# First stage of a fused layer kernel reordered: seven weight chunks moved into the heads, values of tile 0 beside tile 1, one projection piece a step

## Chip, cores, metric

One NeuronCore of a Trainium2 chip (trn2). The metric is the device time of one execution in microseconds (us); the lower, the better. Time before: 1879.2 us, the median of 3 runs (1876.68 to 1882.17).

## The reference

```python
# attention, 16 heads of width 16, two score maps a head
s1 = q1 @ k1.T * scale;  s2 = q2 @ k2.T * scale        # (B=2, H=16, S=2048, S)
a1 = softmax(causal(s1));  a2 = softmax(causal(s2))
lam = exp(sum(lq1*lk1)) - exp(sum(lq2*lk2)) + LAM_INIT
out = (a1 - lam * a2) @ v                              # v of width 32
normed = (out - mean) * rsqrt(var + eps) * (1 - LAM_INIT)
x = layernorm(x + merge(normed) @ Wo)
# feed-forward, ternary weights with a scale for each row
h = silu(lin(x, w1)) * lin(x, w2)
h = gelu(lin(h, h1));  h = gelu(lin(h, h2))
x = layernorm(x + lin(h, w3))
```

x has 2 x 2048 tokens of 256, all in float32; the hidden width is 1024.

## The kernel before, in words

The 4096 tokens are eight tiles of 512. There are three stages: the projection of the first four pairs of heads and of all values; sixteen heads of attention; the rest of the layer, tile by tile. Each engine has its own program, and semaphores tie them together. Nothing is scheduled by a planner: the order is written out by hand.

**First stage** (`project_programs`, from L188). The loops of every engine run over the tiles t = 0..7 and over the pairs m = 0..3. Exact products come from float32r matmuls in three passes (high x high, low x high, high x low), so each input is cut into a high half (ScalarE, `high_x`, L371) and a low half (VectorE, `low_x`, L415). TensorE runs six matmuls for a pair (L525) and, where `value_tiles(t, m)` says so, six for a block s of values (L535). ScalarE copies the pair into one of six `copies` (L389), once the DMAs that read this buffer have landed and VectorE has measured it, and copies the values into `v_sb` (L401), once the store of the values two tiles ago has landed. VectorE takes the largest magnitude (L464). At pairs 2 and 3 it cuts the stacks of the tile before into their halves (`cut_piece`, L566 and L568), for which that tile's placements must have landed, and then runs `low_x(t + 1)`. SyncE's queue, in this order: a store of the pair to `qk_raw` (L309); for pair 0 also twelve placements of 32 KB into the stacks of head 0 (L319); at the end of the tile one load of an early chunk of the feed-forward weights (L291, tiles 0 to 4) and the store of `values` (L326, 1 MB). The loads of xt for later tiles (L282) are issued by ScalarE.

The feed-forward weights are 22 chunks of 128 x 1024. They are rounded to float32r and compared with the original, so that the kernel can tell whether rounding loses anything. Seven early chunks are rounded in the first stage (ScalarE L405, VectorE `compare`, L424); the other fifteen as thirty half chunks in the heads, two a head (`load_half` on SyncE, L1005; `round_half` on VectorE, L1384 and L1386). There is a single staging buffer for halves: `load_half(n)` waits until half n - 1 is compared.

**Heads** (`attention_programs`). A head has four query tiles, and its work is 36 steps: steps 0 to 2 belong to tile 0, 3 to 9 to tile 1, 10 to 20 to tile 2, 21 to 35 to tile 3. For each step TensorE computes the scores (L1196) into one of three PSUM slots, ScalarE the exponentials (L1152), GpSimd the mask on the diagonal, and three steps later TensorE weighs the values with them (L1226). The sums of a tile lie in one of two banks, `sums_ps[t % 2]`; at the end of a tile VectorE transposes them out (`take_sums`, L1402) and finishes the tile.

The pairs of heads 4 to 7 are projected inside heads 0 to 10, as 32 parts, three a head, behind tiles 1, 2 and 3. A part is four **pieces** of TensorE work (L1275), put behind the weighings of the steps that `PIECES_AT` lists. A part lies in the bank that its tile does not use: it can begin once VectorE has emptied that bank, and the first weighing of the next tile, which goes into this bank, waits until VectorE has copied the part out (`take_part`, L1347, semaphore `part_copied`). The weights and inputs of the parts are loaded at the start of head 0 (L1054, L1021).

The order of VectorE in a head before: tile 0, take_part 1, set_rest_bound, tile 1, measure_part 1, eight cuts for the next head, take_part 2, tile 2, measure_part 2, eight cuts, round_half, take_part 3, tile 3, measure_part 3, round_half. The order of SyncE: wait for the scores of the head before, `load_head(h + 1)` (26 DMAs: the shift rows L622, the stacks L592 and the ones L595, 4 MB in all), `load_values`, `store_part` of the last part, `store_rest`, `load_half(2 * h)`, `store_part` 1 and 2, `store_ahead`, `load_half(2 * h + 1)`.

The waits of the two weighings that matter, on TensorE:

```python
if blocks[0] == 0:
    pe.wait_ge(sums_bank_free, NT * h + t + 1)
    part = part_of(h, t - 1) if t > 0 else part_of(h - 1, NT - 1)
    if h < GENERAL and part is not None and part >= 0:
        pe.wait_ge(part_copied, part + 1)
```

Of the kernel before, what the change touches and what calls it, by code (L numbers as in the profile page):

```python
# [6 lines left out]
F32 = mybir.dt.float32  # L7
# [4 lines left out]
ALU = mybir.AluOpType  # L12
# [46 lines left out]
EARLY_CHUNKS = 7  # L59
LAYERS = 2 * HC  # L60
UNSAFE_AT = EARLY_CHUNKS + 2 * (CHUNKS - EARLY_CHUNKS)
# [15 lines left out]
def layer_kernel(nc, x, xt, wqk, wv, wo, lq1, lk1, lq2, lk2, ffn, scales, s3, out):  # L77
# [7 lines left out]
    with ExitStack() as ctx:  # L85
        def sb(name, shape, dt=F32):
# [5 lines left out]
            scales=sb("scales", [PARTS, 4, HC]), counts=sb("counts", [PARTS, 2 * CHUNKS]), wide_col=sb("wide_col", [PARTS, 2]),  # L92
# [15 lines left out]
        with ExitStack() as weights:  # L108
# [4 lines left out]
            with Room(nc, "heads") as room:  # L113
                heads = first_head_buffers(room)
                project = project_programs(nc, ctx.enter_context(Room(nc, "proj")), keep, whole, heads, xt, wqk, wv, (lq1, lk1, lq2, lk2), ffn, (scales, s3),
# [72 lines left out]
def project_programs(nc, sem_room, keep, rounded, heads, xt_in, wqk_in, wv_in, lam_in, ffn, ffn_s, qk_raw, values, shift, ones, later_credits):  # L188
# [5 lines left out]
    scales, s3 = ffn_s  # L194
    M_TILES = FIRST_PAIRS
    BANKS = 4
    COPIES = 6
    STAGES = 2
# [4 lines left out]
    with Room(nc, "proj") as room:  # L203
        copies = [room.sb(f"copies{n}", [PARTS, TILE]) for n in range(COPIES)]
        v_sb = [room.sb(f"v{u}", [PARTS, HEADS, SUBS, VALUE_DIM]) for u in range(2)]
        stage = [room.sb(f"stage{n}", [PARTS, CHUNK]) for n in range(STAGES)]
# [23 lines left out]
        w_loaded = [sem_room.sem(f"w_loaded{n}") for n in range(STAGES)]  # L230
# [17 lines left out]
        w_rounded = sem_room.sem("w_rounded")  # L248
        compared = sem_room.sem("compared")
# [34 lines left out]
        CHUNK_AT = 1  # L284
        VALUE_WEIGHTS_AT = M_TILES - 1
        X_AT = M_TILES - 2
        CUT_AT = {M_TILES - 2: "q", M_TILES - 1: "k"}

        def sync_program(sp):
            def load_w(k):  # L290
                sp.dma_start(stage[k % STAGES][:, :], ffn[k]).then_inc(w_loaded[k % STAGES], 16)  # L291

            for t in range(2):
                load_x(sp, t)
            for k in range(STAGES):
                load_w(k)
# [8 lines left out]
            for t in range(TILES):  # L305
                for m in range(M_TILES):
# [17 lines left out]
                    if SUBS - 1 in value_tiles(t, m):  # L324
                        sp.wait_ge(v_copied, SUBS * t + SUBS)
                        sp.dma_start(values[:, :, bass.ts(t, SUBS), :].rearrange("h p s d -> p h (s d)"),  # L326
                                     v_sb[t % 2][:, :, :, :].rearrange("p h s d -> p h (s d)")).then_inc(v_stored[t % 2], 16)
# [8 lines left out]
            sp.wait_ge(compared, EARLY_CHUNKS)  # L336
# [28 lines left out]
        def scalar_program(act):  # L365
# [11 lines left out]
            for t in range(TILES):  # L377
                for m in range(M_TILES):
# [3 lines left out]
                    if m == 0 and 1 <= t < LAST:  # L382

                        act.wait_ge(v_projected, SUBS * t)
                        load_x(act, t + 1)
# [7 lines left out]
                    for s in value_tiles(t, m):  # L393
                        if s == 0:

                            act.wait_ge(ones_done, 2)
                            if t >= 2:
                                act.wait_ge(v_stored[t % 2], 16 * (t // 2))
                                act.wait_ge(v0_copied, t - 1)
                        act.wait_ge(v_projected, SUBS * t + s + 1)  # L400
                        nc.scalar.copy(v_sb[t % 2][:, :, s, 0:VALUE_DIM - 1], v_ps[s][:, :, 0:VALUE_DIM - 1]).then_inc(v_copied, 1)  # L401
                    if m == CHUNK_AT and t < EARLY_CHUNKS:

                        act.wait_ge(w_loaded[t % STAGES], 16 * (t // STAGES) + 16)
                        nc.scalar.copy(rounded[:, t, :], stage[t % STAGES][:, :]).then_inc(w_rounded, 1)  # L405
                    if m == X_AT and t < LAST:
                        high_x(t + 1)
# [4 lines left out]
        def vector_program(dve):  # L412
# [7 lines left out]

            def compare(k):

                dve.wait_ge(w_rounded, k + 1)
                nc.vector.scalar_tensor_tensor(stage[k % STAGES][:, :], rounded[:, k, :].bitcast(F32), 1.0, stage[k % STAGES][:, :],  # L424
                                               ALU.mult, ALU.not_equal, accum_out=keep["counts"][:, k:k + 1]).then_inc(compared, 1)
# [22 lines left out]
            for n in range(M_TILES):  # L448
# [7 lines left out]
                                           -1.0 / VALUE_DIM, wv_raw[:, :, :], ALU.mult, ALU.add).then_inc(wv_centred, 1)  # L456
            dve.wait_ge(wv_high_done, 1)
            nc.vector.tensor_tensor(wv[1][:, :, :], wv_raw[:, :, :], wv[0][:, :, :].bitcast(F32), ALU.subtract).then_inc(wv_ready, 1)
            for t in range(TILES):
                for m in range(M_TILES):  # L460
# [5 lines left out]
                    if m == CHUNK_AT and t < EARLY_CHUNKS:  # L466
                        compare(t)
# [7 lines left out]
                    if m in CUT_AT and t > 0:  # L475
# [6 lines left out]
                    if m == X_AT + 1 and t < LAST:  # L482
                        low_x(t + 1)
# [7 lines left out]
            dve.wait_ge(compared, EARLY_CHUNKS)  # L491

        def tensor_program(pe):
# [16 lines left out]
            for t in range(TILES):  # L510

                pe.wait_ge(xt_ready, t + 1)
                for m in range(M_TILES):
# [14 lines left out]
                    for s in value_tiles(t, m):  # L528
                        if t == 0:
                            pe.wait_ge(wv_ready, 1)  # L530
                        else:
                            pe.wait_ge(v_copied, SUBS * (t - 1) + s + 1)
# [11 lines left out]
def pair_rows(qk_raw, m):  # L544

    return qk_raw[2 * m:2 * m + 2].rearrange("h w s d n -> (h w s d) n")
# [1706 lines left out]
```

## Time and profile before

| | us |
|---|---|
| median of 3 runs | 1879.2 |
| time of the profiled execution | 1877.55 |
| its span in the trace | 1875.6 |
| TensorE matmul busy | 1826.3 (97%) |
| ScalarE busy | 1392.0 (74%) |
| VectorE busy | 999.0 (53%) |
| GpSimd busy | 228.6 (12%) |
| mean granted TensorE clock | 0.993 of full speed |

The span runs from the first to the last instruction; the execution's time is 2 us more. Busy times count an engine's own work; matmuls are pipelined, so a busy TensorE is not TensorE at its peak. A DMA's issue is an instruction of the queue that issues it (SPq is SyncE's), and its duration is how long that queue was held; the time to landing counts from the start of the issue.

### The profile page before, as it was taken

How to read it: one execution, taken by the hardware profiler on the slowest of the kernel's cores; microseconds unless marked ns; L12 is line 12 of the kernel's file. 1: busy time of each engine (PE TensorE's matmuls, PEld its weight loads, DVE VectorE, ACT ScalarE, POOL GpSimd, SP SyncE). 2: the span in 40 equal slices, each digit the busy share in tenths (PEclk: the TensorE clock that was granted, in tenths of full speed). 3: DMA queues.
4: the chain of work that ended last, by engine and by line, in shares of the span. 5: the costliest groups of instructions: out<-in, count | busy, mean ns of one | idle time of the engine just before them, and what ended most of it. 6: DMA issues, size and time to landing. Idle time of an engine off the chain costs nothing.

```text
span 1875.6 us, 31920 instructions
## 1 busy us (share of the span) xinstructions
PE 1826.3 (97%) x12748; PEld 1030.8 (55%) x12748; DVE 999.0 (53%) x1971; ACT 1392.0 (74%) x1670; POOL 228.6 (12%) x310
## 2 busy tenths in 40 slices
PE   7889999999999999999999999999999999999998
PEld 5653333333333333333333335888888888888886
DVE  4555556555655664566445655454545454636343
ACT  4448999999999999999999997454545454535442
POOL 3010211111111112111211121000000000000000
PEclk9989999999999999999999999999999999999999
DMA  7767644674376357534563411001000101010000
GB/s 228 236 197 171 138 87 102 140 140 93 93 150 126 82 119 142 108 79 89 116 106 68 84 56 41 26 12 34 12 34 12 34 12 34 12 34 24 1 12 13
DMA packets 134053, 154.62 MB, mean 82 GB/s; under 512 B 75572, under 2 KB 102836, under 8 KB 126260
## 3 DMA queue, kind: packets, MB, share of 16 engines
q1 hardware_dynamic: 132312, 148.30, 35.0%
q10 hardware_dynamic: 1584, 4.20, 0.7%
q8 instruction: 103, 1.69, 0.4%
q14 instruction: 54, 0.44, 0.1%
HBM read 110.25 MB, written 39.06 MB: 80 GB/s over the span
## 4 chain that ended last, share of the span: by engine, by line
PE 88%; DVE 5%; ACT 4%; SPq 2%; issue 1%; DMA 1%; ACTq 0%; DVEq 0%; PEldq 0%
PE attn_sums_ps L1226 25%; PE split_hid_ps L1888 25%; PE attn_s_ps L1196 18%; PE split_hid_ps L1872 6%; PE attn_sums_ps L1275 3%; PE split_y_ps L1905 3%; ACT attn_probs L1152 3%; PE split_y_ps L1830 2%; PE proj_v_ps L535 2%; PE proj_qk_ps L525 1%; SPq L319 1%; DVE attn_raw L1402 1%; PE split_turn_ps L1818 1%; DVE attn_raw L1413 1%; ACT proj_xt_high L371 0%
## 5 line engine op out<-in xcount | busy, mean ns | idle before, releaser
L1152 ACT ACTIVATE attn_probs<-attn_s_ps 128x1024 f32<-128x1024 f32 x1088 | 1006.0, 1131 | 24.5 <-PE attn_s_ps L1196 23.0
L1226 PE MATMUL attn_sums_ps<-attn_probs,heads_v 128*32 128x512 f32 (+3 forms) x5120 | 588.5, 541 | 0.0
L1196 PE MATMUL attn_s_ps<-heads_q,heads_k 50*128 50x512 f32 (+3 forms) x2560 | 441.0, 422 | 6.7 <-DVE heads_q L1328 3.4
L1196 PEld LDWEIGHTS attn_s_ps<-heads_q,heads_k 50*128 50x128 f32 x2560 | 207.4, 185 | 413.8 <-ACT attn_probs L1152 340.2
L1982 ACT ACTIVATE split_whole<-split_hid_ps,scales 128x512 f32<-128x512 f32 x128 | 88.3, 690 | 274.1 <-PE split_hid_ps L1888 273.9
L1121 POOL TENSOR_SCALAR_AFFINE_SELECT attn_probs<-attn_probs 128x512 f32<-128x512 f32 x256 | 175.2, 696 | 846.5 <-ACT attn_probs L1152 846.5
L1888 PE MATMUL split_hid_ps<-split_hid_b,ffn_r 128*128 128x512 f32 x1024 | 240.6, 392 | 0.0
L1888 PE MATMUL split_hid_ps<-split_hid_a,ffn_r 128*128 128x512 f32 x1024 | 238.1, 391 | 0.0
L1888 PEld LDWEIGHTS split_hid_ps<-split_hid_a,ffn_r 128*128 128x128 f32 x1024 | 190.1, 188 | 41.0 <-DVE split_hid_a L2155 1.3
L1888 PEld LDWEIGHTS split_hid_ps<-split_hid_b,ffn_r 128*128 128x128 f32 x1024 | 189.8, 188 | 38.0
L1226 PEld LDWEIGHTS attn_sums_ps<-attn_probs,heads_v 128*32 128x32 f32 x5120 | 107.8, 108 | 181.6 <-issue 142.6
L1402 DVE STREAM_TRANSPOSE attn_raw<-attn_sums_ps 128x512 f32<-128x512 f32 x64 | 45.8, 716 | 272.4 <-PE attn_sums_ps L1226 271.9
L2167 DVE TENSOR_TENSOR split_hid_a<-split_whole,split_hid_a 128x512 fp32r<-128x512 f32 x64 | 44.3, 693 | 179.2 <-ACT split_hid_a L1985 179.2
L1872 PE MATMUL split_hid_ps<-split_xt,ffn_r 128*128 128x512 f32 x512 | 119.2, 392 | 0.4 <-PEq L185 0.4
L1967 ACT ACTIVATE split_gate<-split_hid_ps,scales 128x512 f32<-128x512 f32 x64 | 44.1, 688 | 89.8 <-PE split_hid_ps L1872 89.8
L1872 PEld LDWEIGHTS split_hid_ps<-split_xt,ffn_r 128*128 128x128 f32 x512 | 92.4, 188 | 25.5 <-DVE split_whole L2151 4.4
L568 DVE SCALAR_TENSOR_TENSOR heads_k<-heads_spare,low_rows,heads_k_raw 128x512 fp32r<-128x512 f32 x128 | 97.2, 760 | 4.5
L1797 POOL TENSOR_TENSOR split_square<-split_heads 128x512 f32<-128x512 f32 x28 | 31.1, 1129 | 533.0 <-DVE split_head_var L2008 318.6
L568 DVE SCALAR_TENSOR_TENSOR heads_q<-heads_spare,query_rows,heads_q_raw 128x512 fp32r<-128x512 f32 x120 | 92.9, 774 | 4.3
L2167 DVE TENSOR_TENSOR split_hid_b<-split_whole,split_hid_b 128x512 fp32r<-128x512 f32 x64 | 44.2, 690 | 92.4 <-ACT split_hid_b L1985 92.3
L1275 PE MATMUL attn_sums_ps<-ffn_f 128*32 128x256 f32 x1024 | 78.1, 383 | 5.6 <-issue 3.5
L1347 DVE COPY ffn_f<-attn_sums_ps 128x512 f32<-128x512 f32 x32 | 22.1, 692 | 108.3 <-PE attn_sums_ps L1275 108.0
(190 smaller groups left out, 1565.3 us busy)
## 6 DMA issues: line engine op xcount, KB each, us to landing
heads_q_raw<-qk_raw SPq DMA_DIRECT2D x60, 384.0 KB
heads_k_raw<-qk_raw SPq DMA_DIRECT2D x60, 384.0 KB
qk_raw<-proj_copies SPq DMA_DIRECT2D x32, 256.0 KB, 3.3
values<-proj_v SPq DMA_DIRECT2D x8, 1024.0 KB, 7.2
ffn_f<-in_xt SPq DMA_DIRECT2D x16, 512.0 KB, 7.4
qk_raw<-ffn_f SPq DMA_DIRECT2D x32, 256.0 KB, 6.7
heads_k_raw<-ones SPq DMA_DIRECT2D x60, 128.0 KB
heads_v<-values SPq DMA_DIRECT2D x15, 512.0 KB, 18.7
```

What stands on the lines that cost most here:

```text
L568: nc.vector.scalar_tensor_tensor(stack, high.bitcast(F32), low_rows, raw, ALU.mult, ALU.add).then_inc(made, 1)
L1121: pool.affine_select(out=corner, in_=corner, compare_op=ALU.is_ge, fill=0.0, base=0, pattern=[[0, 2 * BATCH], [1, PARTS]], channel_multipl ...
L1152: nc.scalar.activation(weights, side_by_side, ACT.Exp, scale=SCALE).then_inc(exp_done, 1)
L1196: last = nc.tensor.matmul(s_ps[(NU * h + n) % SLOTS][:, s, col:col + width], k_sb[u][rows, b * SEQ + j * PARTS:b * SEQ + (j + 1) * PARTS], ...
L1226: last = nc.tensor.matmul(both, v_sb[u][:, b * KEY_BLOCKS + j, :], alternate[:, :, :, r, :], start=(j == 0), stop=(k == END[t] and j == bl ...
L1275: last = nc.tensor.matmul(sums_ps[(t + 1) % 2][bass.ts(g, D), cols], rest_w[:, m - FIRST_PAIRS, c, bass.ts(g, D)], rest_x[load % 2][:, c, ...
L1402: nc.vector.transpose(raw[:, :, :, :].rearrange("p s g d -> p (s g d)"), sums_ps[t % 2][:, :]).then_inc(sums_bank_free, 1)
L1872: last = nc.tensor.matmul(bank[:, :], weights[w][:, c, m * PARTS:(m + 1) * PARTS], xt[k][:, c, :], start=(c == 0 and k == 0), stop=(c == E ...
L1888: last = nc.tensor.matmul(hid_ps[m % 4][:, :], weights[w][:, c, m * PARTS:(m + 1) * PARTS], hid[k][:, c, :], start=(c == 0 and k == 0), st ...
L1905: last = nc.tensor.matmul(y_ps[s % 2][:, s // 2, :], hid_a[k][:, c, s * PARTS:(s + 1) * PARTS], weights["w3t"][:, c, :], start=(c == 0 and ...
L1982: nc.scalar.activation(gelu, hid_ps[m % 4][:, :], ACT.Gelu, scale=keep[s][:, m:m + 1]).then_inc(gelu_done, 1)
L2167: nc.vector.tensor_tensor(hid[1][:, m, :], whole[m % 2][:, :], hid[0][:, m, :].bitcast(F32), ALU.subtract).then_inc(hid_low, 1)
```

## The change

In the first stage: the early chunks, their loads, roundings and comparisons are gone. The values of tile 0 are projected beside tile 1, two blocks a pair, those of tile 1 as well. `copies` has eight buffers, not six. `high_x` and `low_x` of the next tile come at pair 1 (for tile 2, at pair 2), ahead of the cuts; xt is loaded at the last values of a tile. The last two tiles are cut in head 0's beginning, not one. The loads of the rest weights and inputs go to tile 7, behind its placements. In the heads: 44 half chunks, three a head (head 0 two), the first of them behind tile 0; seven cuts, then nine, not eight and eight; the measure of part 3 goes behind tile 0 of the next head. The pieces in tile 1 stand behind the weighings of steps 4, 5, 6, 7.

```diff
-            if t in (0, LAST):
-                return list(range(SUBS)) if m == M_TILES - 1 else []
-            return list(range(SUBS * m // M_TILES, SUBS * (m + 1) // M_TILES))
+            if t == 0:
+                return []
+            if t == 1:
+                return [(m // 2, s) for s in range(SUBS // 2 * (m % 2), SUBS // 2 * (m % 2 + 1))]
+            if t == LAST:
+                return [(t, s) for s in range(SUBS)] if m == M_TILES - 1 else []
+            return [(t, s) for s in range(SUBS * m // M_TILES, SUBS * (m + 1) // M_TILES)]
...
-    COPIES = 6
+    COPIES = 8
...
-        X_AT = M_TILES - 2
+        X_AT = 1
...
-                    if m == M_TILES - 1 and t + STAGES < EARLY_CHUNKS:
-
-                        sp.wait_ge(compared, t + 1)
-                        load_w(t + STAGES)
...
+                    if (t, m) == (LAST, 0):
+                        load_rest_weights(sp, whole_w, wqk_in, rest_w_loaded)
+                        for i in range(2):
+                            load_rest_x(sp, whole_w, xt_in, i, rest_x_loaded)
...
+                        if s == SUBS - 1 and tile + 2 < TILES:
+
+                            load_x(act, tile + 2)
...
-                    if m == X_AT and t < LAST:
+                    if m == (X_AT if t != 1 else X_AT + 1) and t < LAST:
                         high_x(t + 1)
...
+                    if m == (X_AT if t > 1 else X_AT + 1) and 1 <= t < LAST:
+                        low_x(t + 1)
-                    if m in CUT_AT and t > 0:
+                    if m in CUT_AT and 0 < t < LAST:
...
-                    if m == X_AT + 1 and t < LAST:
-                        low_x(t + 1)
...
-        PIECES_AT = {1: (3, 4, 4, 5), 2: (11, 12, 14, 16), 3: (22, 23, 26, 32)}
+        PIECES_AT = {1: (4, 5, 6, 7), 2: (11, 12, 14, 16), 3: (22, 23, 26, 32)}
...
-                load_half(2 * h)
-                for t in range(1, NT - 1):
-                    store_part(part_of(h, t))
+                first_half = HALVES_A_HEAD * h - 1
+                if not first:
+                    load_half(first_half)
+                store_part(part_of(h, 1))
+                load_half(first_half + 1)
+                store_part(part_of(h, 2))
+                load_half(first_half + 2)
                 store_ahead(h, last)
-                load_half(2 * h + 1)
...
+                first_half = HALVES_A_HEAD * h - 1
                 tile(h, 0)
+                if not first:
+                    measure_part(part_of(h - 1, 3))
+                    round_half(first_half)
                 take_part(part_of(h, 1))
                 set_rest_bound(h)
                 tile(h, 1)
                 measure_part(part_of(h, 1))
-                cut_stacks(h + 1, 1 - u, range(0, CUTS // 2))
+                round_half(first_half + 1)
+                cut_stacks(h + 1, 1 - u, range(0, EARLY_CUTS))
                 take_part(part_of(h, 2))
                 tile(h, 2)
                 measure_part(part_of(h, 2))
-                cut_stacks(h + 1, 1 - u, range(CUTS // 2, CUTS))
-                if 2 * h < HALVES:
-                    round_half(2 * h)
+                cut_stacks(h + 1, 1 - u, range(EARLY_CUTS, CUTS))
+                round_half(first_half + 2)
                 take_part(part_of(h, 3))
                 tile(h, 3)
-                measure_part(part_of(h, 3))
-                if 2 * h + 1 < HALVES:
-                    round_half(2 * h + 1)
```

`EARLY_CUTS` is 7 and `HALVES_A_HEAD` 3; `load_rest_weights` and `load_rest_x` issue the DMAs of L1054 and L1021.

## Rows read from the trace of the kernel before

**Rows 1.** Busy time by stage: stretch, length, busy time and instructions by engine, clock, DMA share, GB/s
```profile
0.00:126.83 126.83, 98.83 (x386) 76.60 (x386) 64.60 (x110) 53.61 (x86) 21.16 (x23) 0.96 0.75 227
126.83:199.30 72.47, 69.49 (x568) 25.75 (x568) 39.13 (x70) 63.48 (x69) 9.74 (x15) 0.91 0.60 145
199.30:836.30 637.00, 634.41 (x5734) 222.91 (x5736) 370.82 (x691) 629.72 (x681) 110.42 (x162) 1.00 0.56 115
836.30:1157.70 321.40, 317.23 (x2492) 109.75 (x2485) 175.50 (x354) 314.03 (x342) 56.17 (x82) 1.00 0.42 81
```

**Rows 2.** TensorE's waits, 0 to 160 us: total us, times, longest
```profile
PE proj_qk_ps L525 <- DVE proj_xt_low L415: 15.2, 6, 2.9
...
PE attn_sums_ps L1275 <- issue: 3.0, 1, 3.0
PE proj_v_ps L535 <- DVE proj_wv_low L458: 2.9, 1, 2.9
```

**Rows 3.** Timeline of SyncE's queue, first stage: start us, us, instruction
```profile
18.22 4.70 SPq L319 DMA_DIRECT2D heads_q_raw<-proj_copies  x6
...
104.76 0.46 SPq L326 DMA_DIRECT2D values<-proj_v  x1
...
119.23 0.45 SPq L326 DMA_DIRECT2D values<-proj_v  x1
...
132.70 0.45 SPq L326 DMA_DIRECT2D values<-proj_v  x1
...
140.20 0.63 SPq L622 DMA_DIRECT2D heads_q_raw<-shift  x2
```

**Rows 4.** Timeline of TensorE: first scores of head 0, its weighing of step 21
```profile
126.83 0.97 PE L1196 MATMUL attn_s_ps<-heads_q,heads_k 50*128 50x512 f32 x8 [3.38 <-DVE heads_q L1328]
...
177.69 1.06 PE L1226 MATMUL attn_sums_ps<-attn_probs,heads_v 128*32 128x512 f32 x8
```

**Rows 5.** Loads of half chunks (line L1005): head 2, head 5, then all thirty
```profile
L1005 SPq DMA_DIRECT2D heads_spare<-in_ffn x1: 10051/10051/10051, 280.2 to 280.2; - x1
...
DMA to landing us min/median/max: 15.4/15.4/15.4
...
L1005 SPq DMA_DIRECT2D heads_spare<-in_ffn x1: 338/338/338, 466.1 to 466.1; - x1
...
DMA to landing us min/median/max: 15.7/15.7/15.7
...
L1005 SPq DMA_DIRECT2D heads_spare<-in_ffn x30: 338/346/12679, 151.2 to 1078.0; - x30
...
DMA to landing us min/median/max: 2.4/8.8/19.8
```

**Rows 6.** Timeline of VectorE in head 5: copy of a part, two cuts, cast and comparison
```profile
470.07 0.69 DVE L1347 COPY ffn_f<-attn_sums_ps 128x512 f32<-128x512 f32 x1 [2.87 <-PE attn_sums_ps L1275]
...
500.03 0.42 DVE L566 CAST heads_spare<-heads_k_raw 128x512 fp32r<-128x512 f32 x1
...
501.27 0.43 DVE L566 CAST heads_spare<-heads_q_raw 128x512 fp32r<-128x512 f32 x1
...
510.02 0.43 DVE L1384 CAST ffn_r<-heads_spare 128x512 fp32r<-128x512 f32 x1
510.48 0.69 DVE L1386 SCALAR_TENSOR_TENSOR heads_spare<-ffn_r,heads_spare 128x512 f32<-128x512 f32 x1
```

**Rows 7.** Timeline of TensorE: the weighing of step 10 in heads 2 and 5
```profile
286.16 1.06 PE L1226 MATMUL attn_sums_ps<-attn_probs,heads_v 128*32 128x512 f32 x8
...
477.06 1.06 PE L1226 MATMUL attn_sums_ps<-attn_probs,heads_v 128*32 128x512 f32 x8
```

**Rows 8.** Two stretches of 4 us, columns as in rows 1
```profile
133.90:137.90 4.00, 4.00 (x24) 1.25 (x24) 3.32 (x7) 2.05 (x2) 0.00 (x0) 0.50 0.99 293
475.40:479.40 4.00, 4.00 (x48) 1.66 (x48) 2.69 (x6) 4.00 (x5) 0.63 (x1) 1.00 0.97 245
```

**Rows 9.** TensorE's waits, 160 to 1110 us: total us, times, longest
```profile
PE attn_sums_ps L1275 <- DVE attn_raw L1402: 2.1, 9, 0.4
```

More of the change, by code:

```diff
@@ L392, in scalar_program @@
                         nc.scalar.copy(wv[0][:, :, :], wv_raw[:, :, :]).then_inc(wv_high_done, 1)
-                    for s in value_tiles(t, m):
+                    for tile, s in value_tiles(t, m):
                         if s == 0:
                             act.wait_ge(ones_done, 2)
[L397 to L405, printed above, removed]
-                    if m == X_AT and t < LAST:
+                            if tile >= 2:
+                                act.wait_ge(v_stored[tile % 2], 16 * (tile // 2))
+                                act.wait_ge(v0_copied, tile - 1)
+                        act.wait_ge(v_projected, SUBS * tile + s + 1)
+                        if s == SUBS - 1 and tile + 2 < TILES:
+                            load_x(act, tile + 2)
+                        nc.scalar.copy(v_sb[tile % 2][:, :, s, 0:VALUE_DIM - 1], v_ps[s][:, :, 0:VALUE_DIM - 1]).then_inc(v_copied, 1)
+                    if m == (X_AT if t != 1 else X_AT + 1) and t < LAST:
                         high_x(t + 1)
@@ L456, in vector_program @@
                                            -1.0 / VALUE_DIM, wv_raw[:, :, :], ALU.mult, ALU.add).then_inc(wv_centred, 1)
+            low_x(1)
             dve.wait_ge(wv_high_done, 1)
@@ L546, in pair_rows, with rest_chunks, load_rest_x, load_rest_weights @@
     return qk_raw[2 * m:2 * m + 2].rearrange("h w s d n -> (h w s d) n")
+def rest_chunks(whole_w):
+    return [whole_w[:, k, :] for k in range(CHUNKS - 4, CHUNKS)]
+def load_rest_x(eng, whole_w, xt_in, n, loaded):
+    i, t = REST_LOADS[n]
+    eng.dma_start(rest_chunks(whole_w)[n % 2], xt_in[t]).then_inc(loaded[n % 2], 16)
+def load_rest_weights(eng, whole_w, wqk_in, loaded):
+    eng.dma_start(rest_chunks(whole_w)[2].rearrange("p (m n) -> p m n", m=HEAD_PAIRS - FIRST_PAIRS), wqk_in[FIRST_PAIRS:HEAD_PAIRS].rearrange("m p n -> p m n")).then_inc(loaded, 16)
 def set_bound(nc, dve, keep, i, big_reduced, steps):
@@ L890, in attention_programs @@
         big_ready, big_reduced, bound_steps = (begun[name] for name in ("big_ready", "big_reduced", "bound_steps"))
-        late_chunks = [whole_w[:, k, :] for k in range(CHUNKS - 4, CHUNKS)]
+        late_chunks = rest_chunks(whole_w)
         rest_x = [late_chunks[u].rearrange("p (c n) -> p c n", c=EC) for u in range(2)]
@@ L916, in attention_programs @@
         CUTS = len(CUT_ORDER)
-        HALVES = 2 * (CHUNKS - EARLY_CHUNKS)
+        EARLY_CUTS = 7
         def half_chunk(n):
             k, half = divmod(n, 2)
-            return EARLY_CHUNKS + k, bass.ts(half, PIECE)
+            return k, bass.ts(half, PIECE)
         def part_of(h, t):
@@ L1052, in head @@
             def head(h, u, first, last):
-                if first:
-                    sp.dma_start(late_chunks[2].rearrange("p (m n) -> p m n", m=HEAD_PAIRS - FIRST_PAIRS), wqk_in[FIRST_PAIRS:HEAD_PAIRS].rearrange("m p n -> p m n")).then_inc(rest_w_loaded, 16)
-                    for n in range(2):
-                        load_rest(n)
                 if last:
@@ L1386, in round_half @@
                 nc.vector.scalar_tensor_tensor(stage, rounded[:, k, cols].bitcast(F32), 1.0, stage, ALU.mult, ALU.not_equal,
-                                               accum_out=keep["counts"][:, EARLY_CHUNKS + n:EARLY_CHUNKS + n + 1]).then_inc(compared, 1)
+                                               accum_out=keep["counts"][:, n:n + 1]).then_inc(compared, 1)
             def sum_counts():
@@ L1569, in rest_of_first @@
             def rest_of_first():
-                add_shift(2)
-                begun["wait_placed"](dve, TILES - 1)
-                for i, name in enumerate(("q", "k")):
-                    cut_piece(nc, dve, heads[f"{name}_raw"][0][:, bass.ts(TILES - 1, TILE)], heads[name][0][:, bass.ts(TILES - 1, TILE)], spare[:, 0, :],
-                              keep["low_rows"][:, i:i + 1], cut_high, i, cut_done)
-                add_shift(3)
+                for t in range(2):
+                    piece = TILES - 2 + t
+                    begun["wait_placed"](dve, piece)
+                    for i, name in enumerate(("q", "k")):
+                        cut_piece(nc, dve, heads[f"{name}_raw"][0][:, bass.ts(piece, TILE)], heads[name][0][:, bass.ts(piece, TILE)], spare[:, 0, :],
+                                  keep["low_rows"][:, i:i + 1], cut_high, 2 * t + i, cut_done)
+                    add_shift(2 + t)
                 finish_query_rows(0)
```

57 lines of the change are left out of this document (18 added, 39 removed).

## The prediction

> **What bounds the kernel now.** I read the table by stage first [rows 1]. The first stage (projection) takes 126.8 us; heads 1 to 10, with a part of the later projection behind three of their four tiles, take 637.0 us, 63.7 us each, with ScalarE busy 629.7 us and TensorE 634.4 us; heads 11 to 15 are bound by ScalarE. The last stage (from 1157.7 us, 718 us) is untouched by the change, and I cost it at nothing. So a wait that stops TensorE in a head for longer than the two or three exponentials that lie ready goes onto the end.
>
> Second, TensorE's waits up to the first pieces: 15.2 us for the low half of xt, in six waits, and 3.0 us at the first piece, for the load of the rest weights [rows 2]. The new order aims at these.
>
> Third, SyncE's queue. It places one tile after the other and is full: the stores of `values` of tiles 5, 6 and 7 are issued 14.5 and 13.5 us apart [rows 3], though no early chunk is loaded there any more, and the last stands at 132.7 us, long after the head's first scores at 126.8 us [rows 4]. So this queue is a second bound of the stage, just behind TensorE.
>
> Fourth, where in a head VectorE meets SyncE. This decides the forecast. The first half chunk of a head is loaded behind the stacks of the next head. It is issued at 280.2 us in head 2, holds SyncE for 10.1 us and lands 15.4 us after its issue; in head 5 it is issued at 466.1 us and lands 15.7 us later; head 0's, issued at 151.2 us, has the longest landing of all thirty, 19.8 us [rows 5]. Before, VectorE wants this half only after all sixteen cuts, some 30 us later than it will after the change, and the wait is never seen.
>
> **The change, part by part.**
>
> *Half chunks in the heads.* Seven whole chunks leave the first stage, and the heads take three halves each (head 0 two) in place of two. Fourteen more halves are 14 times (0.43 + 0.69) us on VectorE [rows 6], 16 us in all; VectorE was busy 371 of 637 us, so the work itself costs nothing. But its place does. In heads 1 to 14 VectorE now runs: tile 0, the measure of the last part, **round_half(first_half)**, then take_part of part 1, then tile 1. SyncE still issues that half behind load_head, load_values and the stores of the head before. In heads 1 to 10 part 1 lies in the bank in which tile 2 is summed: the weighing of step 10 waits for `part_copied`. So the chain is: half lands, cast and comparison 1.2 us, copy of the part 0.7 us [rows 6], weighing of step 10. In head 5 the half lands at 466.1 + 15.7 = 481.8, the copy ends at 483.7, and the weighing now stands at 477.06 [rows 7]: 6.6 us of stall. In head 2 it is 280.2 + 15.4 + 1.9 = 297.5 against 286.16: 11.3 us. These stand near the two ends of the ten (6.6 to 11.9 us); the same subtraction in all ten gives 98 us. The lead of the scores hides about 0.3 us of each (3 us). Heads 11 to 14 have no part in the bank; there the next thing late would be the transposition of tile 1, wanted only at step 21, and I cost them at nothing.
>
> *Clock.* TensorE idles for 7 to 12 us in each of these heads. In 4 us at a granted 0.50 it gets through 24 matmul records, in 4 us at 1.00 through 48 [rows 8]. The lower level is 1.2 GHz. Head 0, where TensorE had stood idle before its start and at the piece, had a mean granted clock of 0.91 over 72.5 us, so 13 us of it at the lower level [rows 1]. Bounds: none of it behind the stall (0 us), or 10 us (5 us lost). I take half: 2.5 us a head, 25 us.
>
> *Second and third half, fewer early cuts.* The second half is issued when the first is compared (about 32 us into the head) and is there by 36 us; VectorE then has seven cuts at 1.24 us [rows 6], is free at 46 us and copies part 2, which step 21, by then at 53 us, waits for. Covered by some 6 us; without that cover it would cost what is missing.
>
> *Pieces.* Of tile 1 the pieces move from behind steps 3, 4, 4, 5 to 4, 5, 6, 7. The first waits for the bank of tile 0, 2.1 us in nine waits [rows 9]. One piece a step spreads the same matmuls. Between nothing and 0.7 us a head, all that ScalarE idles in heads 1 to 10 (637.0 - 629.7 us); I take 0.4 us, a gain of 4 us.
>
> *First stage.* low_x moves ahead of the cuts, so TensorE's 15.2 us go; with them goes the pair of early casts and comparisons, which were covered. What is late next is SyncE. Its placements of tile 0 still begin at 18.2 us, behind the memsets [rows 3]. Tiles 0 and 1 take it to about 41 us (two value stores within tile 1). From there I count 13.5 us a tile, the lower spacing shown, since chunk loads are gone; the upper one is 14.5. Tile 7 carries the three rest loads as well, about 1.5 us: the last value store is issued at 41 + 6 x 13.5 + 1.5 = 123.5 us and lands 6 to 8 us later, at 131. Before, load_head began at 140.2; now at about 131. TensorE, freed from the waits, with eight copy buffers of slack, ends its last projection at about 105 us: 126.8 - 3.4 [rows 4] - 15.2 for the waits and - 3.4 for two stretches at the lower clock that came behind them. The 2.9 us before the first values [rows 2] go too, but ScalarE waits for the first value store at tile 2, which gives 2 to 4 us back. Head 0 can start 20 us earlier.
>
> *Head 0 gives most of that back.* Its piece at step 4 waits for rest weights issued near 118 us, about 6 us of stall. Then VectorE, after tile 1, waits for half 0. That half landed at 151.2 + 19.8 = 171.0, 30.8 us after load_head began. Now the rest loads no longer lie in front of it, so 29 us after 131: 160. Then round 1.2, seven cuts 8.7, copy of part 2 0.7: step 21 can be weighed at 170.7, plus 2 us of clock, 172.7. Now it stands at 177.7 [rows 4]. Gain of the whole front: **5 us**, between 12 (a faster queue) and a loss of 4 (14.5 us a tile).
>
> **Sum.** 1877.6 us is the profiled execution's own time (span 1875.6); the median of the runs shown is 1.6 us above it. 1877.6 - 5 + 98 - 3 + 25 - 4 = 1988.6, or **1989 us**.
>
> One rule of the Trainium skill speaks against this forecast: the page "DMA: Bandwidth & Descriptors", on the two cost components of a DMA, has about 2.0 us fixed plus bytes over 436 GB/s. By it the 256 KB half would be there 2.6 us after its issue and the stall would be gone; the rows of heads 2 and 5 show 15.4 and 15.7 us, so I take it as true only of a queue with nothing in front (the shortest landing of these loads is 2.4 us).
>
> **Rivals.**
>
> 1. *Faster: the half is there in time.* The point is step 10 of each head, 22 us after the head's first exponential. If the half landed before about 20 us, all ten stalls would vanish and so would head 0's long wait. Then only the earlier start counts: 20 to 22 us for the front and 4 for the pieces, 1852 us. For it: half loads on an empty queue are quick. Against: nothing in the change shortens what is in front of this load, and SyncE itself hangs 10.1 us in the issue. Chance 0.06.
>
> 2. *Stalls, but smaller.* Landing a few us sooner because the queues are emptier, and the clock staying high: 5 us a head and a front of -10 give 1877.6 + 50 - 10 = 1918. Range 1890 to 1945. Chance 0.12.
>
> 3. *Worse: the lateness runs on.* If the second half also lands late, part 2 is copied after step 21 wants it, and a head is held twice: 6 us more in ten heads, 2050 us. Against: by then the queue is empty. Chance 0.07.
>
> 4. *It cancels.* Front and stalls even out within 0.3%. That needs 2 us a head. Chance 0.02.
>
> The forecast has 0.73: its own range is 1950 to 2020 (stalls 85 to 110, clock 5 to 40, front -12 to +4).
>
> **How the numbers follow.** A measurement of this kernel can tell about 0.3%, 5.6 us. Range 1940 to 2025: the forecast and the upper part of rival 2. Faster is rival 1 and a little of rival 2: 0.07; same 0.02; slower 0.91.
>
> **What would show it.** Right: VectorE with one wait of 12 to 20 us in each of heads 1 to 14, ended by the load of `heads_spare`; TensorE waiting at the first weighing of tile 2 in ten heads, for the copy of part 1, with ScalarE idle 8 us and more; a granted clock below 1.00 in heads 1 to 10; period 73 to 76 us there and 62.5 us in heads 11 to 14; no wait for xt_low except one near tile 3; head 1 starting a few us before 199 us. Wrong: heads 1 to 10 still near 63 us apart, which would be rival 1; or periods near 69 us at full clock, rival 2; or two stalls in a head, rival 3. If head 1 starts at 180 us, half 0 was not what held head 0.

## The result and the profile after

The median of four runs after the change is 2008.1 us (2003.5 to 2010.1), beside 1878.4 us for the kernel before on the same chip: a ratio of 1.0684 [1.0658, 1.0711]. The forecast was 1989 us, with a range of 1940 to 2025: the sign and the size were right, and two terms of the sum (the front and the pieces) were not. The profiled execution took 2009.8 us, span 2008.0 us, 132.4 us more than before.

The page of the kernel after, its span and busy slices (in tenths; PEclk is the granted clock):

```profile
span 2008.0 us, 31939 instructions
PE 1849.1 (92%) x12748; PEld 1034.8 (52%) x12748; DVE 1006.3 (50%) x1999; ACT 1387.3 (69%) x1663; POOL 228.3 (11%) x310
PEclk9988898898898898898999999999999999999999
```

The stages of after, with the columns of [rows 1]. The second line begins with head 0's first exponential, the third with head 1's, the fourth with head 11's:

```profile
0.00:110.90 110.90, 96.10 (x388) 75.13 (x388) 54.48 (x92) 45.96 (x79) 19.89 (x22) 0.97 0.70 205
110.90:205.60 94.70, 68.75 (x566) 24.49 (x564) 42.15 (x77) 63.45 (x70) 9.81 (x16) 0.84 0.56 136
205.60:966.30 760.70, 660.42 (x5734) 229.61 (x5736) 380.68 (x721) 632.61 (x681) 110.15 (x162) 0.92 0.48 100
966.30:1287.00 320.70, 316.86 (x2492) 109.75 (x2484) 179.31 (x362) 314.05 (x342) 57.19 (x82) 1.00 0.44 85
1287.00:2008.00 721.00, 706.98 (x3580) 595.82 (x3576) 349.71 (x750) 331.21 (x495) 31.22 (x28) 0.99 0.07 22
```

Read against [rows 1], heads 1 to 10 went from 637.0 to 760.7 us: 123.7 of the 132.4 us. Head 1 starts at 205.6 instead of 199.3 us, 6.3 more. The remaining 2.4 us are at the end (from the start of the last exponential to the end of the span 724.6 us, before 722.2). Within heads 1 to 10 the table splits the 123.7 us: the same 5734 matmul records were busy 660.4 us instead of 634.4, 26.0 us more at a granted clock of 0.92, and TensorE was idle 100.3 us instead of 2.6, 97.7 more. VectorE and ScalarE have the work they had.

What that idle time is, by the waits of TensorE and of VectorE over the whole run (total us, times, longest):

```profile
PE attn_sums_ps L1218 <- DVE ffn_f L1339: 115.0, 11, 14.7
PE proj_qk_ps L506 <- DVE proj_xt_low L404: 8.3, 4, 3.8
```

```profile
DVE ffn_r L1376 <- DMA heads_spare<-in_ffn: 284.5, 20, 21.1
```

L1218 is the weighing, L1339 the copy of a part, L1376 the rounding of a half chunk. One wait of 14.7 us is in head 0 and ten, together 100.3 us, are in heads 1 to 10. The chain can be seen in head 5, the head of [rows 7]. SyncE's queue, the issues of the first and of the second half:

```profile
519.68 12.31 SPq L1003 DMA_DIRECT2D heads_spare<-in_ffn  x1
...
541.12 0.45 SPq L1003 DMA_DIRECT2D heads_spare<-in_ffn  x1
```

VectorE in the same head, with the idle time before an instruction in brackets:

```profile
538.25 0.43 DVE L1376 CAST ffn_r<-heads_spare 128x512 fp32r<-128x512 f32 x1 [17.54 <-DMA heads_spare<-in_ffn]
538.71 0.69 DVE L1378 SCALAR_TENSOR_TENSOR heads_spare<-ffn_r,heads_spare 128x512 f32<-128x512 f32 x1
...
539.33 0.69 DVE L1339 COPY ffn_f<-attn_sums_ps 128x512 f32<-128x512 f32 x1
...
545.96 0.43 DVE L1376 CAST ffn_r<-heads_spare 128x512 fp32r<-128x512 f32 x1 [1.85 <-DMA heads_spare<-in_ffn]
```

TensorE and ScalarE in it, the weighing of step 10 and the exponentials after it:

```profile
540.16 1.94 PE L1218 MATMUL attn_sums_ps<-attn_probs,heads_v 128*32 128x512 f32 x8 [9.40 <-DVE ffn_f L1339]
```

```profile
542.92 1.94 ACT L1144 ACTIVATE attn_probs<-attn_s_ps 128x1024 f32<-128x1024 f32 x2 [10.20 <-PE attn_s_ps L1188]
```

The half lands 18.5 us after its issue, the cast follows at once, the copy of part 1 is queued behind it on VectorE though the part is ready, and TensorE resumes when that copy is done. VectorE had been free for the half since 520.7 us; the last piece of part 1 was done by 527.0, 12.3 us ahead of its copy. The weighing takes 1.94 us where it took 1.06 [rows 7]. Four windows of this head, up to the stall, the stall, what follows it, and the rest, show how long the lower clock lasts:

```profile
508.70:530.80 22.10, 22.06 (x214) 8.32 (x212) 7.04 (x14) 21.48 (x25) 6.69 (x10) 1.00 1.02 177
530.80:540.20 9.40, 0.04 (x4) 0.07 (x6) 1.92 (x5) 1.93 (x3) 0.00 (x0) 0.73 0.66 156
540.20:549.50 9.30, 9.30 (x52) 2.64 (x52) 6.91 (x16) 3.88 (x4) 0.00 (x0) 0.53 0.36 116
549.50:585.60 36.10, 36.10 (x314) 12.20 (x312) 22.59 (x40) 36.04 (x39) 4.62 (x7) 1.00 0.13 28
```

Behind the stall TensorE works for 9.3 us at 0.53, which is the level of 1.2 GHz nearly throughout, and ScalarE is busy 3.88 us of them: the scores come too slowly for it. That is the second price of the stall.

### The profile page after: what moved, and what is told of

Its sections match the earlier page's. It is cut to its first block, busy times and chain, and to the rows that moved or that the text cites. A ratio compares the mean times of both kernels' runs of the same rounds, so it can differ in the third digit from the quotient of the medians.

```text
span 2008.0 us, 31939 instructions
## 1 busy us (share of the span) xinstructions
PE 1849.1 (92%) x12748; PEld 1034.8 (52%) x12748; DVE 1006.3 (50%) x1999; ACT 1387.3 (69%) x1663; POOL 228.3 (11%) x310
## 4 chain that ended last, share of the span: by engine, by line
PE 76%; DMA 10%; SPq 8%; DVE 3%; ACT 2%; issue 1%; ACTq 0%; DVEq 0%; PEldq 0%
PE split_hid_ps L1882 23%; PE attn_sums_ps L1218 21%; PE attn_s_ps L1188 15%; DMA heads_spare<-in_ffn 9%; PE split_hid_ps L1866 6%; PE split_y_ps L1899 3%; PE split_y_ps L1824 2%; SPq L592 2%; SPq L589 2%; PE attn_sums_ps L1267 2%; PE proj_qk_ps L506 2%; SPq L977 1%; PE proj_v_ps L516 1%; ACT attn_probs L1144 1%; SPq L313 1%
## 5 line engine op out<-in xcount | busy, mean ns | idle before, releaser
L1218 PE MATMUL attn_sums_ps<-attn_probs,heads_v 128*32 128x512 f32 (+3 forms) x5120 | 603.5, 553 | 115.0 <-DVE ffn_f L1339 115.0
L1188 PE MATMUL attn_s_ps<-heads_q,heads_k 50*128 50x512 f32 (+3 forms) x2560 | 450.6, 429 | 3.4 <-ACT attn_probs L1144 3.4
L1218 PEld LDWEIGHTS attn_sums_ps<-attn_probs,heads_v 128*32 128x32 f32 x5120 | 109.0, 109 | 300.2 <-issue 262.6
L1376 DVE CAST ffn_r<-heads_spare 128x512 fp32r<-128x512 f32 x44 | 19.1, 433 | 285.9 <-DMA heads_spare<-in_ffn 284.5
L1267 PE MATMUL attn_sums_ps<-ffn_f 128*32 128x256 f32 x1024 | 84.4, 403 | 11.2 <-DVE attn_raw L1394 11.2
```

What stands on the lines that cost most here:

```text
L1188: last = nc.tensor.matmul(s_ps[(NU * h + n) % SLOTS][:, s, col:col + width], k_sb[u][rows, b * SEQ + j * PARTS:b * SEQ + (j + 1) * PARTS], ...
L1218: last = nc.tensor.matmul(both, v_sb[u][:, b * KEY_BLOCKS + j, :], alternate[:, :, :, r, :], start=(j == 0), stop=(k == END[t] and j == bl ...
L1267: last = nc.tensor.matmul(sums_ps[(t + 1) % 2][bass.ts(g, D), cols], rest_w[:, m - FIRST_PAIRS, c, bass.ts(g, D)], rest_x[load % 2][:, c, ...
```

## The experiments

Nine kernels were run. Each ratio is to the kernel before on the same chip; smaller than 1 is faster.

**1. The load moved alone.** The place of the first half's load in SyncE's order against everything else in the change.

```diff
             def head(h, u, first, last):
+                first_half = HALVES_A_HEAD * h - 1
+                if not first:
+                    load_half(first_half)
                 if last:
...
-                first_half = HALVES_A_HEAD * h - 1
-                if not first:
-                    load_half(first_half)
                 store_part(part_of(h, 1))
```

> The changed kernel with one difference: the first half chunk of a head is loaded ahead of the stacks of the next head, not behind them; VectorE's order stays. My theory (VectorE waits for a load that lies behind 4 MB in SyncE's queue, and the copy of part 1 waits behind VectorE): the ten stalls at step 10 vanish, heads 1 to 10 take 63 to 64 us each in place of 76.1, and the time is about 1873 us, 135 below the changed kernel. Rival (VectorE itself is too full with three halves a head): heads stay above 70 us, and the time above 1940.

Measured: 1894.0 us, 1.0098 [1.0082, 1.0114]. In head 2 the half is there 2.5 us after its issue, all ten stalls at step 10 are gone, and heads 1 to 10 take 642.9 us at full clock:

```profile
111.20:204.90 93.70, 67.51 (x566) 23.91 (x562) 41.59 (x77) 63.43 (x68) 10.47 (x15) 0.84 0.58 140
204.90:847.80 642.90, 634.36 (x5734) 224.53 (x5736) 385.66 (x721) 630.17 (x681) 114.62 (x162) 1.00 0.56 118
```

One load moved ahead of 22 issues on its queue (the 18 of load_head, not 26 as the text ahead of the prediction has it, and four more) is worth 114 us (2008.1 to 1894.0). It also moves ahead of SyncE's wait for the scores: in head 2 it is issued 5.6 us before the head's first exponential, where head 5 of the kernel after issues it 10.9 us behind it. But about 21 us of what I had expected did not come. The first line is head 0: 93.7 us, where it took 71.8 before. Its half 0 still lies behind load_head(1), and VectorE shows it:

```profile
170.81 0.43 DVE L1376 CAST ffn_r<-heads_spare 128x512 fp32r<-128x512 f32 x1 [21.32 <-DMA heads_spare<-in_ffn]
```

The rest is 0.6 us a head more than before: in six of the ten ScalarE has a gap of 0.6 to 1.0 us at step 21, which experiment 2 doesn't have. There the second half is now the late one: VectorE waits 4.7 to 6.7 us for it in each of heads 1 to 10, and the seven cuts and the copy of part 2 stand behind it.

**2. The order of VectorE alone.** The loads stay as in the change; only the roundings go behind the work that others wait for.

```diff
                     measure_part(part_of(h - 1, 3))
-                    round_half(first_half)
...
                 measure_part(part_of(h, 1))
-                round_half(first_half + 1)
...
                 measure_part(part_of(h, 2))
+                if not first:
+                    round_half(first_half)
                 cut_stacks(h + 1, 1 - u, range(EARLY_CUTS, CUTS))
-                round_half(first_half + 2)
+                round_half(first_half + 1)
                 take_part(part_of(h, 3))
                 tile(h, 3)
+                round_half(first_half + 2)
```

> The changed kernel with another difference: the load stays where it is, but VectorE rounds the first half only behind tile 2, the second behind the cuts, the third behind tile 3. My theory: the half lands as late as before (15 us after its issue), nobody waits for it, and heads 1 to 10 take 63 to 64 us: about 1873 us, the same as with the early load. Rival (the third half a head costs time wherever it stands): 1880 to 1900 us.

Measured: 1876.0 us, 0.9988 [0.9979, 0.9997]. Heads 1 to 10:

```profile
196.40:833.00 636.60, 636.26 (x5738) 225.10 (x5736) 388.19 (x721) 628.49 (x682) 117.71 (x162) 1.00 0.57 119
```

Here the half lands as late as before (the slowest half of heads 1 to 10 takes 19.8 us), VectorE has no wait for any half, and TensorE none at step 10. Experiments 1 and 2 mend different ends of the same chain, and either removes the stall: so it needs both, the load behind load_head and the rounding ahead of the copy. And 388 us of work on VectorE (before 371) cost nothing.

**3. The stores of `values` on ScalarE**, with the load of experiment 1: whether the queue of SyncE sets when load_head begins.

```diff
-                    for tile, sub in value_tiles(t, m):
-                        if sub == SUBS - 1:
-                            sp.wait_ge(v_copied, SUBS * tile + SUBS)
-                            sp.dma_start(values[...], v_sb[...]).then_inc(v_stored[tile % 2], 16)
...
                         nc.scalar.copy(v_sb[...], v_ps[...]).then_inc(v_copied, 1)
+                        if s == SUBS - 1:
+                            act.wait_ge(v_copied, SUBS * tile + SUBS)
+                            act.dma_start(values[...], v_sb[...]).then_inc(v_stored[tile % 2], 16)
```

> The kernel with the early load, and besides the 1 MB value stores of the first stage issued by ScalarE, not SyncE. Theory for the front (SyncE's queue bounds the first stage, because the issue behind each value store is held 3 to 5 us): the placements of a tile follow each other in about 12 us, not 14.7, load_head begins near 125 us, not 140, and the time is 8 to 15 us below the kernel with the early load alone. Rival (the 16 DMA engines themselves are full): spacing 14 to 15 us as before, and no gain, or a loss by ScalarE's waits.

Measured: 1881.0 us, 1.0021 [1.0010, 1.0032], 13 us faster than experiment 1, within the 8 to 15 us expected, though load_head begins at 128.9 us and not near 125. On SyncE's queue of this kernel the rest weights' load and the first instruction of load_head:

```profile
117.60 0.58 SPq L542 DMA_DIRECT2D ffn_f<-in_wqk  x1
...
128.91 0.61 SPq L618 DMA_DIRECT2D heads_q_raw<-shift  x2
```

and in the kernel after:

```profile
126.81 0.58 SPq L543 DMA_DIRECT2D ffn_f<-in_wqk  x1
...
129.90 0.51 SPq L321 DMA_DIRECT2D values<-proj_v  x1
140.08 0.60 SPq L619 DMA_DIRECT2D heads_q_raw<-shift  x2
```

With eight stores less on the queue load_head begins 11.2 us sooner. ScalarE's gap at head 0's first piece falls from 11.3 us in experiment 1 to 2.1 us, and head 1 starts at 194.8 us instead of 204.9. The long wait at step 21 stays (15.3 us of ScalarE), as half 0 is still behind load_head(1).

**4. The pieces alone**, on the kernel before.

```diff
-        PIECES_AT = {1: (3, 4, 4, 5), 2: (11, 12, 14, 16), 3: (22, 23, 26, 32)}
+        PIECES_AT = {1: (4, 5, 6, 7), 2: (11, 12, 14, 16), 3: (22, 23, 26, 32)}
```

> The kernel before with only the pieces of tile 1 moved, from behind steps 3, 4, 4, 5 to 4, 5, 6, 7. Theory: heads 1 to 10 get 0.4 us shorter each (63.7 to 63.3 us), the time falls by about 4 us (0.2%), and head 0 perhaps gains 1 to 2 us at the load of its weights. Rival: the gaps only move to later steps, and the time stays within 1 us.

Measured: 1875.8 us, 0.9999 [0.9990, 1.0008]. The small gaps of ScalarE in tile 1 move by some exponentials, and heads 1 to 9 take 63.5 to 63.8 us each. All ten:

```profile
196.60:832.30 635.70, 635.70 (x5734) 225.23 (x5736) 370.44 (x691) 628.78 (x681) 110.44 (x162) 1.00 0.57 115
```

TensorE's 2.6 us of waiting at the pieces [rows 1] are gone, and the ten heads are 1.3 us shorter, less than the times can tell. The forecast's 4 us were not there.

**5 and 9. The stall filled.** To measure what the lower clock costs behind the stall, TensorE transposes the identity 44 times (then 64 times) into a free score slot ahead of the wait for the copy at step 10 of heads 1 to 10. Nobody reads the results; nothing is left out.

```diff
                     if h < GENERAL and part is not None and part >= 0:
+                        if t == 2 and h > 0:
+                            n = LAST_UNIT[k + LAG] + 1
+                            pe.wait_ge(exp_done, NU * h + n - SLOTS + 1)
+                            for _ in range(FILLERS):
+                                nc.tensor.transpose(s_ps[(NU * h + n) % SLOTS][:, 0, 0:PARTS], keep["ident"][:, :], keep["ident"][:, :])
                         pe.wait_ge(part_copied, part + 1)
```

> The changed kernel, with 44 transposes of the identity (their result is never read) put into the stall at step 10 of heads 1 to 10, ahead of TensorE's wait for the copy of part 1. The stall itself stays as long; TensorE only has something to do in it. My theory (behind each stall the granted clock is at its lower level for some us, which costs 2 to 2.5 us a head): the granted clock stays 1.00 in heads 1 to 10 and each is 2 to 2.5 us shorter, about 1985 us in all. Rival (what a head loses beyond the stall is the lost lead of the scores, not the clock): the time stays at 2008 us.

> As the run with 44 transposes in each stall, but with 64. There TensorE still idled 3.9 us a head behind the transposes, and the clock fell all the same in most heads (mean 0.96). At 0.14 us each the further 20 fill 2.8 us more. Theory (the clock, which falls only after idle time, is what a head loses beyond its stall): mean granted clock in heads 1 to 10 near 1.00, a head 73.5 us or less (after the change 76.1, with 44 transposes 75.0), about 1985 us. Rival (the transposes only take up time): heads stay at 75 us or more.

Measured: 2001.0 us, 1.0653 [1.0619, 1.0688], with 44; 1993.7 us, 1.0610 [1.0584, 1.0635], with 64. Both filled too little: 44 take 4.99 us and leave 3.9 us of stall in a head, 64 take 7.18 us (0.11 us each, not the 0.14 expected) and leave 2.5. The second one in heads 1 to 5, one line a head:

```profile
204.80:276.60 71.80, 70.80 (x643) 29.45 (x641) 38.03 (x72) 63.19 (x69) 11.01 (x16) 1.00 0.49 104
276.60:353.50 76.90, 73.13 (x642) 29.97 (x640) 38.03 (x72) 63.32 (x70) 10.82 (x16) 0.96 0.50 103
353.50:428.10 74.60, 72.14 (x642) 29.76 (x640) 38.11 (x72) 63.32 (x70) 10.62 (x16) 0.98 0.48 100
428.10:503.10 75.00, 72.18 (x642) 29.76 (x640) 37.94 (x72) 63.22 (x70) 11.14 (x16) 0.98 0.50 106
503.10:575.90 72.80, 70.74 (x645) 29.40 (x643) 39.14 (x74) 63.29 (x70) 11.64 (x17) 1.00 0.49 103
```

Take from each length the 63.7 us of a head before, the 7.2 us of transposes and TensorE's idle time (length less busy). At a clock of 1.00 nothing is left (-0.1 and -0.2 us); at 0.98 1.2 and 1.3 us are left; at 0.96 2.2 us. Heads 6 to 10 agree: nothing is left in the one at 1.00, 1.2 to 2.9 us in the four at 0.96 to 0.98. In the kernel after, at 0.92, the same subtraction leaves 23.4 us in ten heads, 2.3 a head (760.7 - 637.0 - 100.3). So what a head loses beyond its stall comes with the lower clock and is nothing without it; the rival, the lost lead of the scores (those that lie ready when the stall begins), would show at 1.00 too, since no scores are made during the transposes either. The loss is not in proportion to the mean clock: in the kernel after a part of the lower clock lies in the stall itself (0.73 in the window of head 5's stall), where it costs nothing. Over the ten heads the filling gave back 1.2 us a head, not the 2 and more I had expected (76.1 to 74.9), since the lower clock still came in most heads. A filling that leaves no idle time wasn't tried.

Experiment 3 holds an unplanned comparison. In its heads 3 and 5 TensorE stops at step 21 for the same 1.48 us; the clock falls behind the one stop and not behind the other:

```profile
323.10:389.60 66.50, 65.02 (x578) 22.72 (x576) 38.18 (x72) 63.13 (x69) 10.53 (x16) 0.97 0.54 112
454.40:519.30 64.90, 63.42 (x578) 22.51 (x576) 38.62 (x74) 63.10 (x69) 11.42 (x17) 1.00 0.56 114
```

The head at 0.97 is 1.6 us longer, and TensorE's busy time is 1.6 us longer. This is the price of the lower clock with an equal stall.

**6, 7 and 8. Toward a better version.** Experiment 7 asks how much of head 0's wait is the place of half 0: experiment 1, with half 0 loaded ahead of load_head(1).

```diff
             def head(h, u, first, last):
-                if not first:
-                    load_half(first_half)
+                load_half(first_half if not first else 0)
...
-                load_half(first_half + 1)
+                if not first:
+                    load_half(first_half + 1)
```

> The early load of the first run, in head 0 too: its first half is loaded ahead of the stacks of head 1. Theory (the 15.7 us that ScalarE idles at step 21 of head 0 are VectorE's wait for this half, then for the stacks): this gap falls to about 6 us, as with the late rounding, and the time from 1894 to about 1884 us. Rival (the gap is the stacks' landing alone): it stays above 13 us.

Measured: 1883.5 us, 1.0023 [1.0008, 1.0037]. ScalarE's gap at step 21 falls from 15.5 to 9.0 us, head 0 from 93.7 to 86.3. I had expected some 6 us of gap. VectorE no longer waits for a half there but, twice, for the stacks that it is to cut:

```profile
158.34 0.43 DVE L563 CAST heads_spare<-heads_k_raw 128x512 fp32r<-128x512 f32 x1 [7.61 <-DMA heads_k_raw<-ones]
...
170.47 0.43 DVE L563 CAST heads_spare<-heads_k_raw 128x512 fp32r<-128x512 f32 x1 [6.83 <-DMA heads_k_raw<-ones]
```

So the rest of this gap is the landing of load_head(1). Experiment 2 has the same two waits (6.8 and 6.0 us) and a gap of 6.2 us.

Experiment 6 is experiment 2 with the stores of experiment 3; experiment 8 also issues the three rest loads two tiles sooner:

```diff
-                    if (t, m) == (LAST, 0):
+                    if (t, m) == (LAST - 2, 0):
                         load_rest_weights(sp, whole_w, wqk_in, rest_w_loaded)
```

> The late rounding of the second run together with the value stores on ScalarE's queue. Theory (two separate causes: VectorE's order costs the heads, SyncE's queue costs the front): load_head begins near 129 us, the rest weights are there when head 0 wants them, and step 21 of head 0 no longer waits; head 1 starts near 182 us, heads 1 to 10 take 63.5 us; about 1862 us, 0.7 to 0.8% below the kernel before. Rival (the front is bound elsewhere, by the stacks of head 1): head 1 starts at 190 us or later, and the time is above 1870.

> The kernel with late rounding and the value stores on ScalarE, with the three rest loads two tiles earlier, at tile 5 and not 7. Theory: the gap of about 2 us at the first piece of head 0 goes, and load_head begins up to 1.5 us earlier; 2 us below the kernel without this, near the limit of what can be told. Rival: the 1.5 MB delay xt or the stores of tile 5 or 6 by as much, and nothing is gained.

Measured: 1861.3 us, 0.9901 [0.9878, 0.9924], for experiment 6, as expected but for a gap of 5.1 us that is left at step 21 of head 0; and 1856.3 us, **0.9873 [0.9851, 0.9895]**, for experiment 8, 5.0 us less where I had expected 2. This one beats the kernel before by 1.3% and the kernel after by some 150 us. Its SyncE queue, the rest weights and load_head (127.2 us in experiment 6):

```profile
95.93 0.59 SPq L542 DMA_DIRECT2D ffn_f<-in_wqk  x1
...
124.89 0.61 SPq L618 DMA_DIRECT2D heads_q_raw<-shift  x2
```

Its head 0 and its heads 1 to 10:

```profile
110.70:180.00 69.30, 69.30 (x566) 25.43 (x564) 41.06 (x73) 63.75 (x69) 10.00 (x15) 0.89 0.57 138
180.00:815.00 635.00, 635.00 (x5734) 225.06 (x5736) 388.23 (x721) 628.47 (x681) 117.68 (x162) 1.00 0.56 119
```

In head 0 TensorE never waits, neither at the piece nor at step 21, and head 1 starts at 180.0 us, 19.3 us sooner than before. This is what the new order of the first stage can give once its queue lets it.

## Why the prediction was right, and where it was not

**The whole.** The profiled execution took 21.2 us more than the sum (21.4 by the span and its rows): 11.3 by the front, 6.7 by idle time in heads 1 to 10 (97.7 where stall, lead and pieces had 91), 1.0 by the clock, 2.4 by the end. All four err the same way.

**The stall (98 us).** Right, by its own steps. The ten waits are 100.3 us, 7.9 to 11.6 each, and VectorE waits 16.0 to 20.0 us for the first half in each of heads 1 to 14. Head 5 was forecast 6.6 us from the old landing of 15.7 us; it had 9.4, since the half now takes 18.5 us. The subtraction held because the load's place on the queue hadn't changed, and so its landing time could be read from the trace of before. Experiments 1 and 2 show that both links are needed. One reading was off without changing the sum: VectorE wants the half 12 us into the head, and took it 55 us into it before [rows 6], 43 us apart and not "some 30".

**The lead (-3) and the pieces (-4).** Experiment 4 puts the pieces at next to nothing: the 7 us that ScalarE idles in ten heads were the ceiling, and with the same matmuls spread the ten heads are 1.3 us shorter in the trace and the time is the same. It does remove TensorE's waits at the pieces, and these are the 2.6 us by which the stalls (100.3) and the growth of idle time (97.7) differ. For the lead nothing is left: no run measures it by itself, but length, stalls and clock add up without it.

**The clock (+25).** 26.0 us by the busy time of the same 5734 records, or 23.4 us as what the ten heads lost beyond their stalls; in experiment 4 the busy time fills the 2.6 us between the two without any fall of the clock. The term was half of a bound, so the closeness is partly luck. That the loss comes with the clock, the heads of experiment 9 and the pair in experiment 3 show.

**The second half.** In five heads VectorE waited for it, 1.1 to 3.1 us (1.85 in head 5), and part 2 was still copied in time: TensorE has no wait at step 21 of heads 1 to 10. Rival 3 fell. Heads 11 to 14 kept 62.3 us. Rivals 1 and 2 fell as well: the queue in front of the load was no shorter.

**The front (-5).** Here it failed; it came out at +6.3 us, outside its own range of -12 to +4. The step is the one on SyncE's queue: "From there I count 13.5 us a tile, the lower spacing shown, since chunk loads are gone". It was the upper one. The store of tile 1, from which I counted, on SyncE's queue (the last one, at 129.90 us, is shown in experiment 3):

```profile
41.85 1.08 SPq L321 DMA_DIRECT2D values<-proj_v  x1
```

That is 88.1 us for six tiles; less 1.6 us for the rest loads, 14.4 us a tile. The last store then took 10.0 us to land, not 6 to 8. So load_head began at 140.1 us, not 131, and where it had begun before (140.2). A second, smaller step failed as well: with the rest loads no longer in front, half 0 was to land 29 us after load_head began; it took 30.9 us, as it had before (30.8). So it landed at 171.0 us, to a tenth as before. The rest of head 0 follows by the forecast's own steps: 1.2 + 8.7 + 0.7 us later step 21 should be weighed:

```profile
181.68 1.94 PE L1218 MATMUL attn_sums_ps<-attn_probs,heads_v 128*32 128x512 f32 x8 [14.71 <-DVE ffn_f L1339]
```

181.7 instead of 170.7 (172.7 with the clock) forecast and 177.7 before [rows 4]. From there to head 1 it takes 23.9 us at a clock of 0.89, before 21.6 at 1.00; these 2.3 us and the 4.0 make the 6.3. The rest loads were issued at 126.8 us, not 118, so the first piece held ScalarE 11.5 us instead of 6. TensorE's waits for the low half of xt fell only from 15.2 to 8.3 us, and ScalarE waited 15.8 us, in four waits, for the stores of `values`, where I had 2 to 4. Head 0 still started 16.5 us sooner (20 forecast), and TensorE then stood idle for 26 of its 94.7 us. Why each tile took 14.4 us is partly shown: in experiment 3, with the 1 MB stores off the queue of the placements, load_head begins 11 us sooner. How much of that is issue time, how much transfer and how much the wait for the last store's landing was not separated.

**The end (0).** The 2.4 us are not in TensorE's work: its last matmul ends 713.7 us after the start of the last exponential, before 713.5. They lie behind it, among the last instructions of SyncE. Experiments 1, 2, 5, 7 and 9 have the same length (724.2 to 724.5 us), experiments 3, 4, 6 and 8 the one before (722.3 to 722.5), one trace each. No experiment aimed at it, and the cause stays open.

**The page's rule.** The forecast set the trace against the page "DMA: Bandwidth & Descriptors" of the Trainium skill (on the two cost components of a DMA), from which it estimated 2.6 us for the half. The trace agrees where nothing is in front of the load, with 2.5 us in experiment 1, and differs behind load_head, with 18.5 us in head 5 of the kernel after; there the measurement decides.

## What to carry to other kernels

Where a step is moved forward on one engine, look for what it waits for and where that stands on its own queue: the landing time can be read from the trace before, and it doesn't shrink because the consumer is sooner. Keep work whose result nobody awaits (here a rounding) behind the work that others await (here a copy that frees a bank). And look for a full queue behind the engine that seems to bound a stage: here the freed TensorE brought head 1 only 2.9 us forward (196.4 us, experiment 2) while the queue stayed as it was, and 19.3 us once it was relieved (experiment 8).

## What the runs showed of the hardware

The issue itself can be held: the first half's issue held SyncE 12.3 us in head 5 behind the issues of load_head, and 0.33 us in head 2 of experiment 1, ahead of them. A short issue doesn't mean a short landing: in head 5 of the kernel before it held SyncE 0.34 us, and the load landed 15.7 us later [rows 5]. Of the five heads of experiment 9 that are shown, the two in which TensorE idled 1.0 and 2.1 us had a mean granted clock of 1.00, the three with 2.5 to 3.8 us had 0.96 to 0.98. But the length of the stop alone doesn't decide it: in experiment 3 one stop of 1.48 us was followed by the lower clock and another was not. A stall of 9.4 us was followed by another 9.3 us at 0.53.
